# A four-layer graph network on one core: the last normalisation moved into the last loop's block, in groups of node tiles

## What is computed

```
x = layernorm(x + L0(x, edge_attr_64))
x = layernorm(x + L1(x))
x = layernorm(x + L2(x))
x = layernorm(x + L3(x, edge_attr_2))
```

```
msg = w[:, None] * (z_src + ez)
x3  = segment_sum(msg, dst)
out = (x + x3 - mean) / sqrt(var + 1e-5)
```

## Time and profile before

| | us |
|---|---|
| median of 3 runs (device time) | 1907.07 |
| lowest, highest | 1906.61, 1913.65 |
| span of the profiled execution | 2674.2 |
| last sum of the loop ends, in that span | 2640.26 |
| engines meet behind the loop; the end block begins | 2640.5; 2646.1 |
| stores issued | 2667.9 to 2670.55 |

### The profile page before, as it was taken

How to read it: one execution, slowest core, us unless ns; L and a number is a source line. 1 busy time by engine, 2 the same in 40 slices (tenths; PEclk the granted TensorE clock), 3 DMA queues, 4 the chain that set the end, 5 groups by cost and what they waited for, 6 DMA issues and landing times. The chain is left out here.

```text
span 2674.2 us, 43621 instructions
## 1 busy us (share of the span) xinstructions
PE 1501.4 (56%) x12903; PEld 1250.3 (47%) x12903; DVE 1423.4 (53%) x3785; ACT 1008.8 (38%) x2221; POOL 1227.4 (46%) x1328
## 2 busy tenths in 40 slices
PE   3555555555555654555555774754134656555795
PEld 2444444434444443344434673753033645444785
DVE  6455555555555554555555787871023534434685
ACT  3333333333333333333333651750003534434683
POOL 2555555555555554545553460546724343444100
PEclk7677777777777767777777787885556777777897
DMA  5222222222222222222221210022201111111100
GB/s 116 54 58 56 58 59 57 59 57 61 57 58 60 56 59 52 60 55 58 59 57 35 62 59 3 2 87 34 35 17 33 37 34 37 32 41 33 40 26 14
DMA packets 125233, 128.69 MB, mean 48 GB/s; under 512 B 80959, under 2 KB 88435, under 8 KB 124840
## 3 DMA queue, kind: packets, MB, share of 16 engines
q0 software_dynamic: 35776, 62.74, 10.4%
q1 hardware_dynamic: 63778, 57.41, 7.8%
q10 hardware_dynamic: 25542, 6.81, 1.1%
HBM read 116.64 MB, written 10.20 MB: 47 GB/s over the span
## 5 line engine op out<-in xcount | busy, mean ns | idle before, releaser
L634 POOL DMA_INDIRECT shared<-kv_tab,idx x784 | 763.2, 974 | 674.3 <-DMA idx<-in_src 459.3
L836 PE MATMUL bank<-key_hot,lo_hot 128*128 128x350 f16 x784 | 220.8, 394 | 586.5 <-DVE count L698 392.4
L836 PEld LDWEIGHTS bank<-key_hot,lo_hot 128*128 128x128 f16 x784 | 59.3, 101 | 703.4 <-issue 690.4
L2282 POOL DMA_INDIRECT count<-att_tab,count x240 | 228.3, 951 | 301.7 <-PE bank L2827 193.4
L698 DVE TENSOR_TENSOR count<-count,bank 128x350 f32 x392 | 205.4, 524 | 109.4 <-issue 73.6
L735 DVE TENSOR_TENSOR acc<-acc,bank 65x64 f32 x98 | 21.3, 217 | 429.2 <-remote 425.8
L779 ACT ACTIVATE expo<-score 128x32 f32<-128x32 f32 x98 | 22.5, 229 | 587.3 <-DVE score L716 566.9
L769 ACT ACTIVATE lo_dist<-iota_neg,tile_lo 128x128 f16<-128x128 f32 x784 | 238.5, 389 | 0.0
L2656 ACT ACTIVATE shared<-shared 128x126 f32<-128x126 bf16 x336 | 144.4, 484 | 172.0 <-PE bank L2804 88.6
L683 DVE TENSOR_SCALAR key_hot<-iota_key,tile_key 128x350 f16<-128x350 f16 x784 | 193.3, 319 | 0.0
L851 PEld LDWEIGHTS bank<-hots,msg 128*65 128x65 f32 x1568 | 183.8, 221 | 0.4 <-DVE msg L725 0.4
(11 more groups left out here) (528 smaller groups left out, 3237.8 us busy)
## 6 DMA issues: line engine op xcount, KB each, us to landing
shared<-in_edge_attr SPq DMA_DIRECT2D x97, 256.0 KB
shared<-lo_tab SPq DMA_DIRECT2D x28, 512.0 KB
shared<-kv_tab,idx POOLq DMA_INDIRECT x784
count<-att_tab,count POOLq DMA_INDIRECT x240
qwin<-q_tab ACTq DMA_DIRECT2D x196, 16.0 KB
kv_tab<-count SPq DMA_DIRECT2D x1, 1600.0 KB, 10.4
idx<-in_src SPq DMA_DIRECT2D x97, 4.0 KB, 1.6
g_edge<-att_tab,count POOLq DMA_INDIRECT x94
```

Source lines behind the costliest of these rows:

```text
L634: nc.gpsimd.indirect_dma_start(kv[:, s, c, :], None, kv_tab, bass.IndirectOffsetOnAxis(ap=idx[:, s, c:c + 1], axis=0)).then_inc(kv_in[s], 16)
L836: last = nc.tensor.matmul(bank[6 + q % 2][:, 0:KC], lo_hot[:, c, :], key_hot[:, c, :], start=i == 0, stop=i == GT - 1)
L2282: nc.gpsimd.indirect_dma_start(ring[s][:, j, 0:D + 2], None, att_tab[1], bass.IndirectOffsetOnAxis(ap=src_i[:, t:t + 1], axis=0)).then_inc ...
```

## The change

Every engine's part of the end is appended to its list in the fast path's block, so the fast path now runs to the stored output before the block closes and the flag is read. The old end block moves inside the general path (functions `last_pe`, `last_dve`, `last_act`, `last_sp`), and runs only if that is taken. What is appended:

- **POOL** (`centre_x`), behind its last gather: it takes the mean over each node's 64 features out of `xrow` by halving additions in two lots of 13 and 12 tiles, then one addition over all 25 tiles.
- **DVE** (`turning_matrix`, `centre_matrix`), ahead of its wait for the last unit's sum: it builds `back` and takes out the mean of each of its rows, so that what PE multiplies out has a mean of nothing. The later reduction over the rows and the subtraction fall away.
- **PE** (`end_pe`): 25 matmuls in groups `ENDS` of 7, 7, 6 and 5 tiles, tiles 18 to 24 first.
- **DVE** (`end_dve`), **ACT** (`end_act`): the same steps as before by these groups, interleaved; ACT loads the table of the root ahead of its first wait.
- **POOL** (`end_pool`) scales the rows of the first three groups, DVE those of the last; **SP** (`end_sp`) stores each group as it is ready, five DMAs in all, and waits for them after the general path's branch (`at_last`).

To have enough semaphores, those of an earlier stage are taken from the short-lived ones and cleared with others at line 1809; there POOL has five range clears in place of four. Behind the loop it has four in place of one. The new code, cut:

```diff
-        begun, slot_free, hot_ok, sum_ok = sem("h_begun"), sem("h_free"), sem("h_hot"), sem("h_sum")
+        begun, slot_free, hot_ok, sum_ok = short_sem("h_begun"), short_sem("h_free"), short_sem("h_hot"), short_sem("h_sum")
...
+        ENDS = [slice(18, NT), slice(0, 7), slice(7, 13), slice(13, 18)]
...
+        def centre_x(pool):
+            for w in HALF:
+                n = w.stop - w.start
+                part = low_hot[:, 0:n * (D // 2)].rearrange("p (t f) -> p t f", t=n)
+                nc.gpsimd.tensor_tensor(part, xrow[:, w, 0:D // 2], xrow[:, w, D // 2:D], ALU.add)
+                pool.drain()
+                f = D // 4
+                while f > 1:
+                    nc.gpsimd.tensor_tensor(part[:, :, 0:f], part[:, :, 0:f], part[:, :, f:2 * f], ALU.add)
+                    pool.drain()
+                    f //= 2
+                nc.gpsimd.tensor_tensor(x_mean[:, w], part[:, :, 0], part[:, :, 1], ALU.add)
+                pool.drain()
+            nc.gpsimd.tensor_scalar(x_mean, x_mean, -1.0 / D, None, ALU.mult)
+            pool.drain()
+            nc.gpsimd.tensor_tensor(xrow[:, :, :], xrow[:, :, :], bc(x_mean, 2, D), ALU.add).then_inc(x_centred, 1)
...
+        def centre_matrix(dve):
+            nc.vector.tensor_reduce(back_mean, back[:, 0:D], AX.X, ALU.add)
+            dve.drain()
+            nc.vector.tensor_scalar(back_mean, back_mean, -1.0 / D, None, ALU.mult)
+            dve.drain()
+            nc.vector.tensor_scalar(back[:, 0:D], back[:, 0:D], back_mean, None, ALU.add)
+
+        def end_pe(pe):
+            pe.wait_ge(acc_done, 1)
+            for k, w in enumerate(ENDS):
+                for j, t in enumerate(range(w.start, w.stop)):
+                    last = nc.tensor.matmul(bank[k][:, j * (D + 1):(j + 1) * (D + 1)], acc[0:ME, t * P:(t + 1) * P], back[0:ME, :], start=True, stop=True)
+                last.then_inc(ends_up, 1)
...
+            for k in range(len(ENDS)):
+                add(k)
+                if k >= 1:
+                    spread_of(k - 1)
+                if k >= 2:
+                    scale(k - 2)
+            spread_of(len(ENDS) - 1)
+            scale(len(ENDS) - 2)
+            scale(len(ENDS) - 1)
+
+        def end_act(act):
+            nc.scalar.activation(root_early, zeros_b[:, 0:1], ACT.Sqrt)
+            for k, w in enumerate(ENDS):
+                act.wait_ge(end_added, k + 1)
+                nc.scalar.activation(total[:, w, :], tmp[:, w, :], ACT.Square).then_inc(end_squared, 1)
+                act.wait_ge(end_var, k + 1)
+                nc.scalar.activation(deg[:, w, 0], stat[:, 3, w], ACT.Sqrt).then_inc(end_root, 1)
+
+        def end_pool(pool):
+            for k, w in enumerate(ENDS[:-1]):
+                pool.wait_ge(end_scale, k + 1)
+                nc.gpsimd.tensor_tensor(qt[:, w, :], tmp[:, w, :], bc(dis[:, w], 2, D), ALU.mult).then_inc(end_scaled, 1)
...
+                    if i == ND - 1:
+                        turning_matrix(dve)
+                        centre_matrix(dve)
                     dve.wait_ge(sum_d, i + 1)
...
                 add_sums(ND)
+                dve.drain().then_inc(acc_done, 1)
+                end_dve(dve)
```

More of the change, by code:

```diff
@@ L1511, in _ @@
                         finish["sp"](sp)
+                    if at_last is not None:
+                        at_last(sp)
                 @block.gpsimd
@@ L2269, in by_dve @@
             return nc.vector.tensor_copy(into, of)
+        ME = D + 4
+        end_row = work_diag[:, 1, :, :].rearrange("p b n -> p (b n)")
+        back = end_row[:, 0:D + 1]
+        mask_of = [end_row[:, P + k:P + k + 1] for k in range(2)]
+        back_mean = end_row[:, P + 2:P + 3]
+        x_mean = end_row[:, P + 4:P + 4 + NT]
+        root_early = end_row[:, P + 3:P + 4]
+        ENDS = [slice(18, NT), slice(0, 7), slice(7, 13), slice(13, 18)]
+        x_centred, acc_done, ends_up, end_added, end_squared, end_var, end_root, end_scale, end_out, end_stored = (
+            short_sem(f"o_{n}") for n in ("x_centred", "sums_complete", "turned", "added", "squared", "variance", "deviation", "factors", "last_rows", "stored"))
@@ L2902, in l3_sp @@
             sp.dma_start(ea2[0:PL, G - 1, :, :], edge_attr_2[full:E, :].rearrange("(p c) k -> p c k", c=C)).then_inc(ea2_in, 16)
[L2904 to L2909, removed]
         back_ok, summed, shift_ok, square_ok, var3, std3, out_ok, stored = (
-            short_sem(f"o_{n}") for n in ("matrix", "summed", "centred", "squared", "variance", "deviation", "rows", "stored"))
+            short_sem(f"g_{n}") for n in ("matrix", "summed", "centred", "squared", "variance", "deviation", "rows", "stored"))
@@ L2912, in build @@
         sevens = [range(t, min(t + RT, NT)) for t in range(0, NT, RT)]
         halves = [slice(0, 2 * RT), slice(2 * RT, NT)]
[L2914 to L2927, removed]
+        fast_stores = 16 * (len(ENDS) + 1)
@@ new lines, in last_pe, with last_dve @@
+        def last_pe(pe):
+            pe.wait_ge(back_ok, 1)
+            for k, ts in enumerate(sevens):
+                for j, t in enumerate(ts):
+                    last = nc.tensor.matmul(bank[k][:, j * (D + 1):(j + 1) * (D + 1)], acc[0:ME, t * P:(t + 1) * P], back[0:ME, :], start=True, stop=True)
+                last.then_inc(summed, 1)
+        def last_dve(dve):
+            dve.drain()
+            turning_matrix(dve)
+            dve.drain().then_inc(back_ok, 1)
+            for k, ts in enumerate(sevens):
+                w = slice(ts[0], ts[-1] + 1)
+                dve.wait_ge(summed, k + 1)
+                ps = bank[k][:, 0:len(ts) * (D + 1)].rearrange("p (t m) -> p t m", m=D + 1)
+                nc.vector.tensor_scalar(stat[:, 0, w], ps[:, :, D], 1e-30, None, ALU.max)
```

151 lines of the change are left out of this document (100 added, 51 removed).

## The result

The changed kernel takes 1897.81 us (median of 13 runs, 1893.33 to 1908.78) against 1914.11 for the kernel before on the same chips (13 runs, 1905.74 to 1918.97): a ratio of **0.9928, 95% interval 0.9908 to 0.9947**, that is 13.8 us less (10.1 to 17.6). The two medians themselves lie 16.3 us apart, and the three runs of before that the forecast counts from had a median of 1907.07; so the saving is taken from the ratio. 12.5 us less were forecast.

A forecast was written before the change was run, and what follows sets the result against it. No engine was full; the end took 33.9 us after the last sum (T). Forecast 0.15 + 1.85 + 13.0 + 0.2 + 0.5 + 5.5 = 21.2, saving 12.7 less 0.2: 1907.07 - 12.5 = 1894.6 us, range 1890.5 to 1900.5.

The forecast's parts named there:

- DVE's list: End block: with PE no longer last, DVE sets the pace, 13.0 us, so the last rows are ready at T+15.0.
- the front of the kernel: Start of the kernel: one more clear at line 1809, 0.2 us taken, ends 0 and 0.5.
- Matrix ahead of the sum: Loop's end: building and centring the turning matrix fits in DVE's wait for PE, 1.9 of 4.2 us, costing nothing.
- PE's start and clock: End's matmuls: PE starts at about T+0.15 at clock 1.00, DVE at T+2.0, all 50 passes end at T+5.6.
- The bound of +1.6: End's matmuls: at half clock the first group comes 1.5 us later, in all +1.6 us at the end.
- POOL's products: Row scaling in the end: contention with DVE's last product puts 0.2 us on the path, ends 0 and 2.7.
- Stores: Five DMAs by SP: the last two groups land some 3.4 us from the issue, at T+18.6.
- Crossing: Two meetings with the flag between, moved behind the last issue: 5.5 us again, bounds 4.3 and 7.0, hiding the landing.
- POOL's means: Behind POOL's last gather: means of x done beside the loop, 0 us taken, ends 0 and 4.
- (a): Rival: the crossing does not stay what it was, or the end scales with the shorter run; about 1898.5 us, chance 0.14.
- (b): Rival: POOL beside DVE, all three products and half of the means' bound on the path; 1899.3 us, chance 0.08.
- (c): Rival: POOL's arithmetic holds DVE, PE runs dry and the loop loses its clock; slower, 1925 us, chance 0.04.

## Why the prediction was right, step by step

The forecast was 1894.6 us with a range of 1890.5 to 1900.5; 1897.81 lies in it, and 0.72% less stands against 0.66% forecast. By its own steps:

- **The whole.** T+21.2 forecast, T+19.7, 19.1 and 19.2 measured, against 33.9 and 33.7. The saving from T on was 14.0 to 14.8 us where the sum has 12.7, and the misses behind it all go one way: DVE's list 1.3 too long, the crossing 0.5 to 1.1. The 0.2 for the front of the kernel is too small to be seen.
- **Matrix ahead of the sum.** 1.9 of 4.2 us: measured 1868.78 to 1870.65, 1.87 us, and 1.90 us of wait left. Right.
- **PE's start and clock.** DVE's first group at T+2.0: measured T+1.95, at 2.4 GHz. Right for what counts. "All 50 passes end at T+5.6" was wrong: T+8.4, T+6.7 and T+8.0 in the three profiles, in which the granted clock fell at T+3.1, T+5.0 and T+3.5. The bound of +1.6 for this did not come about, since only the later passes are slow, and DVE is behind them anyway.
- **DVE's list.** 13.0 us from its start forecast, 11.7 measured (T+1.95 to T+13.7). The mis-sized term is the gaps: 0.7 us were put down for eleven of them, and there were none, since a new part's first operation starts before the last one's end (from one group's clamp to the next 1.76 us, 1874.74 to 1876.50, where I had 1.85 and 0.06). The additions took 6.5 us in place of 7.0, the sums of squares 2.9 in place of 3.2. The waits for ACT were 0.53 and 0.18, as taken.
- **POOL's products.** 0.2 taken, 0.32 measured.
- **Stores.** Landing at T+18.6 forecast, T+16.6 measured. The 3.4 us from the issue were an error of the sum: 5.9 us scaled by 1408 of 3125 rows are 2.7, and 2.8 us from the last issue's start is what it took. Hidden in either case.
- **Crossing.** 5.5 forecast, 5.0, 4.4 and 4.5 measured, inside its bounds, but by another engine than the row of before named. The size was right and the mechanism, PE's branch, was not what set it.
- **POOL's means.** "x must be ready at T, 133 us later" was the step that failed. In a run of normal length the means are done at T-9.7, 12.9 us before they are needed at T+3.2: the cover was a tenth of what I read, since the earlier trace rows come from an execution in which POOL's last gather was issued 141.9 us ahead of T, where the second profile of before has 28.8. It was still enough. The means also took 20.2 us (T-29.9 to T-9.7) where I had 9.4, because 9.1 us of them is the first drain, which stood in the earlier trace rows and was read there as gathers still running. That this drain has a price wherever it stands I did not see, and the sum has no term for it. The change happens to put it beside the loop; without the means it falls on the first meeting and costs 8 us. So the 0 for this term came true by luck.
- **Rivals.** (a) fell: the end does not scale with the run, and the crossing became shorter. (Its own figures give 1897.7 to 1898.2, not 1898.5.) (b) is there at a fifth of its price at most: 0.32 us at the last product and half a microsecond ahead of T, where it had 4.7. Of (c) nothing was seen: while POOL takes the means (1842 to 1860 us) the clock is 0.91, and in the 4 us behind 1.00, the same as in the second profile of before at the same distance from T; over the last 100 us ahead of T it is 0.89 to 0.91 in the changed kernel and 0.89 in before. The two stretches in the changed kernel, columns as above:

```profile
1842.00:1860.00 18.00, 13.73 (x128) 12.64 (x127) 13.99 (x44) 13.43 (x35) 6.94 (x14) 0.91 0.04 6
1860.00:1864.00 4.00, 3.95 (x35) 3.48 (x34) 1.97 (x9) 3.32 (x11) 2.94 (x2) 1.00 0.00 0
```

## What to carry to other kernels

A last stage that stands behind a meeting, a flag and a branch pays for them in full. Behind the last store the same crossing lies beside the landing, and here costs 1.1 to 1.8 us of its 5. It also costs the stage its clock: here PE came out of the crossing at half clock, while a stage that begins at once has its first passes at full clock. When an engine issues indirect DMAs, look for its first drain behind them before work is taken from it or added to it: that drain has a price of its own, 9.1 us here, and should stand where nothing waits. And compare the length of a profiled span with the runs. Where they differ by hundreds of microseconds, the slack of an engine in it is not the slack of a run; the end block, a chain without gathers, was the same within 0.2 us.

## What the runs showed of the hardware

- POOL's first drain behind its indirect DMAs ended 9.07 us after the instruction ahead of it in thirteen profiles and 9.08 in the fourteenth, whether that was a gather's issue, an addition of the means, or a product 41 us after the last gather. Its own record reads 12.5 to 13.8 us in the first two cases, since it begins while gathers are still being issued, and 9.95 in the third; another drain behind it, at the same line, took 0.94, and 0.83 of that lie beside POOL's last product.
- Two of DVE's instructions that met POOL's addition over 1600 elements a partition ended 0.05 to 0.08 us behind it: one over 126 elements took 0.88 us in place of 0.35, one over 64 took 2.38 in place of 0.25. Beside the same addition a reduction over 64 elements and an operation on one element kept their 0.22 and 0.15 us.
- The same compare and branch takes PE 4.35 and 4.15 us in the kernel before, 3.99 with the changed body behind it, and 0.33 to 0.43 with the end ahead of it; DVE's is recorded with 0.07 us in all, yet its next instruction came 3.0 to 3.6 us later in the changed kernel. The length of such a crossing can't be read from one engine's branch.
- TensorE's granted clock fell from 1.00 to 0.50 between T+3.1 and T+5.2 in all the kernels, whether it had been idle since the last sum (T+3.7 and T+4.5 in the two profiles of before) or at work from T+0.1 on (T+3.1, T+5.0 and T+3.5 in those of the changed kernel).
- The DMA of the last 53 rows took SP 1.37 to 1.40 us to issue right behind another of 1280 rows (L2977 in the earlier trace rows), with a third of 1792 rows issued by ACT 1.2 us before, and 0.40 behind one of 768 rows in the changed kernel (line 2403). Which of the two makes the difference no run separates.
